# One slot of a software-pipelined attention, its groups of work in another order on five engines

## The reference

```python
x = x + xattn(layernorm(x), ctx)      # 16 heads of depth 32; q from x, k and v from ctx; softmax over 154
x = x + ffn(layernorm(x))             # 8 experts of 512x512; each token goes through its best 2
```

## Time and profile before

| | us |
|---|---|
| time, median of 3 runs | 1331.4 (1330.66 to 1331.42) |
| span of the profiled execution | 1340.9 |
| PE busy | 1224.7 (91%) |
| DVE busy | 881.3 (66%) |
| POOL busy | 744.6 (56%) |
| ACT busy | 722.1 (54%) |

### The profile page before, as it was taken

The page is one execution under the profiler, slowest core; times in us unless marked ns, Lnnn a source line. Parts: engine busy times, 40 slices in busy tenths (PEclk is TensorE's granted clock), DMA queues, the critical chain, the costliest instruction groups (busy, mean ns, idle before and its releaser), DMA issues. The chain is left out here.

```text
span 1340.9 us, 36001 instructions
## 1 busy us (share of the span) xinstructions
PE 1224.7 (91%) x11024; PEld 735.1 (55%) x11025; DVE 881.3 (66%) x1933; ACT 722.1 (54%) x1040; POOL 744.6 (56%) x980
## 2 busy tenths in 40 slices
PE   8887999998999989999999986869899999999997
PEld 4445665655655655665655654534354555555454
DVE  4657787877868867867877867545445555555454
ACT  4336875775775775775766662624333333334333
POOL 4003555675675675675675674864644445444545
PEclk9879999999989998989989997889999999999999
DMA  8842664584583574583583573967999989998886
GB/s 267 253 135 65 173 176 153 148 254 142 150 258 130 142 241 152 147 262 131 144 237 115 132 215 109 357 221 156 199 177 184 175 173 188 179 172 155 168 165 133
DMA packets 135547, 239.22 MB, mean 178 GB/s; under 512 B 18440, under 2 KB 49416, under 8 KB 134280
## 3 DMA queue, kind: packets, MB, share of 16 engines
q1 hardware_dynamic: 102391, 161.24, 41.2%
q0 software_dynamic: 29808, 67.73, 25.2%
q10 hardware_dynamic: 3232, 8.68, 1.9%
HBM read 112.00 MB, written 101.40 MB: 159 GB/s over the span
## 5 line engine op out<-in xcount | busy, mean ns | idle before, releaser
L1854 PE MATMUL S<-we_s,wq_s 128*128 x1620 | 376.3, 382 | 12.6 <-DVE att L1832 5.8
L1782 POOL DMA_INDIRECT out<-xn,to x135 | 208.9, 1547 | 212.7 <-DMA out<-xn,to 123.6
L1854 PEld LDWEIGHTS S<-we_s,wq_s 128*128 128x128 f16 x1620 | 158.1, 98 | 180.8 <-issue 22.3
L1172 POOL TENSOR_TENSOR we_s<-P_s,we_s 128x1024 f16<-128x1024 f32 x96 | 204.2, 2136 | 65.6 <-ACT we_s L927 65.3
L1793 ACT ACTIVATE wq_s<-PVp 128x512 f16<-128x512 f32 x137 | 81.6, 597 | 272.4 <-PE PVp L1844 247.1
L1252 POOL DMA_INDIRECT dispatched<-xn,idx x128 | 131.7, 1029 | 92.6 <-ACT xn L620 52.1
L975 DVE TENSOR_REDUCE mx_sb<-S 128x6 f32<-128x924 f32 x160 | 171.3, 1111 | 11.3 <-PE S L726 9.1
L708 PE MATMUL W<-we_s,wq_s 128*128 128x512 f16 x512 | 168.7, 409 | 8.7 <-ACT mT L933 5.3
L746 PE MATMUL W<-wo_s,aT_hi 128*128 128x512 f16 x512 | 164.5, 383 | 2.6 <-DVE aT_lo L953 1.4
L1832 DVE SCALAR_TENSOR_TENSOR att<-S,be_s 128x512 f32<-128x512 f32 x135 | 93.3, 691 | 111.0 <-PE S L1854 101.5
L1810 DVE TENSOR_TENSOR wq_s<-PVp,wq_s 128x512 f16<-128x512 f32 x137 | 94.6, 691 | 38.3 <-ACT wq_s L1793 35.1
(11 more groups left out here) (207 smaller groups left out, 2039.8 us busy)
## 6 DMA issues: line engine op xcount, KB each, us to landing
P_s<-dispatched SPq DMA_DIRECT2D x139, 260.5 KB
we_s<-we_s SPq DMA_DIRECT2D x186, 128.0 KB, 6.0
be_s<-in_x SPq DMA_DIRECT2D x16, 1024.0 KB, 9.1
xR_s<-in_x SPq DMA_DIRECT2D x16, 1024.0 KB
out<-xR_s SPq DMA_DIRECT2D x16, 1024.0 KB
...
```

Source lines behind the costliest of these rows:

```text
L1172: e.tensor_tensor(Pst[1][:, r:r + 2, :], exps(n), Pst[0][:, r:r + 2, :], ALU.subtract).then_inc(pldp, 1)
L1782: e.indirect_dma_start(out, bass.IndirectOffsetOnAxis(ap=to[u][:, :], axis=0), yw[u % YW], None, bounds_check=N - 1, oob_is_err=False, com ...
L1854: m = e.matmul(Yp[:, u % 2, :], gT[u % 2][xp][:, k, :], we_s[:, bass.ds(n * WN + (wp * KC + k) * D, D)], start=(c == 0), stop=(c == 11))
```

## The change

The five slot functions list the same calls in another order. No call is added or dropped, no helper, wait, buffer or bank is changed (`not b.last` has only gained brackets). The parts that the prediction speaks of:

```diff
 def pe_slot(e, s):
...
         if on_bm1:
             pe_PV(e, bm1, 6)
+            pe_PV(e, bm1, 7)
...
         if on_bm1:
             pe_AT(e, bm1, 0, s)
-            pe_PV(e, bm1, 7)
         if on_b:
             pe_ST(e, b, 3, s)
+            pe_ST(e, b, 4, s)
         if on_bm1:
             pe_AT(e, bm1, 1, s)
-        if on_b:
-            pe_ST(e, b, 4, s)
         if on_bp1:
             pe_LA(e, bp1, s)
+        if on_b:
+            pe_ST(e, b, 5, s)
         if on_bm1:
             pe_AT(e, bm1, 2, s)
             pe_AT(e, bm1, 3, s)
         if on_b:
-            pe_ST(e, b, 5, s)
             pe_PV(e, b, 0)
             pe_PV(e, b, 1)
...
         if on_bp2:
             pe_XT(e, bp2, 3, s)
-        if on_bm1 and not bm1.last:
+        if on_b:
+            pe_ST(e, b, 9, s)
+        if on_bp1:
+            pe_MX(e, bp1, 0, s)
+        if on_bm1 and (not bm1.last):
             pe_O(e, bm1, 3, s)
             pe_O(e, bm1, 4, s)
             pe_O(e, bm1, 5, s)
         if on_bp2:
             pe_Q(e, bp2, 0, s)
             pe_Q(e, bp2, 1, s)
-        if on_bp1:
-            pe_MX(e, bp1, 0, s)
...
             pe_MX(e, bp1, 4, s)
+        if on_b:
+            pe_PV(e, b, 4)
+        if on_bp1:
+            pe_MX(e, bp1, 5, s)
...
         if on_bp1:
-            pe_MX(e, bp1, 7, s)
-        if on_b:
-            pe_PV(e, b, 4)
-        if on_bp1:
             pe_MX(e, bp1, 8, s)
...
 def act_slot(e, s):
...
             act_EX(e, b, 2)
+            act_PH(e, b, 2)
         if on_bp1:
             act_Qh(e, bp1, 3)
...
+        if on_bp3 and (not bp3.first):
+            act_norm(e, 0, bp3)
+        if on_b:
             act_EX(e, b, 9)
             act_PH(e, b, 8)
             act_PH(e, b, 9)
-        if on_bp3 and not bp3.first:
-            act_norm(e, 0, bp3)
         if on_bp2:
             act_Qh(e, bp2, 0)
         if on_bp3:
             act_NX(e, bp3, 0)
-        if on_bp2:
-            act_Qh(e, bp2, 1)
-            act_WEh(e, bp2)
-        if on_bm2 and not bm2.last:
+            act_NX(e, bp3, 1)
+            act_NX(e, bp3, 2)
+        if on_bm2 and (not bm2.last):
             act_NY(e, bm2, 0)
...
 def dve_slot(e, s):
...
             dve_RB(e, bm3)
-        if on_bp2 and bp2.past(2):
-            dve_SA(e, bp2, 3)
-        if on_b:
-            dve_WEl(e, b)
+            dve_RM(e, bm3)
+        if on_b:
             dve_Ql(e, b, 2)
         if on_bm1:
             dve_PL(e, bm1, 1)
+        if on_bm2:
+            dve_NM(e, bm2, 3)
         if on_b:
             dve_Ql(e, b, 3)
...
 def sp_slot(e, s):
...
+        if on_bp3 and bp3.past(3):
+            sp_XA(e, bp3)
         if on_b:
             sp_KV(e, b)
-        if on_bp1:
-            sp_WL(e, bp1)
-        if on_bp3 and bp3.past(3):
-            sp_XA(e, bp3)
-        if on_b:
             sp_RS(e, b)
             sp_WW(e, b)
+        if on_bp1:
+            sp_WL(e, bp1)
```

More of the change, by code:

```diff
@@ L1429, in pe_slot @@
             pe_MX(e, bp1, 3, s)
-        if on_bm1 and not bm1.last:
-            pe_O(e, bm1, 6, s)
+            pe_MX(e, bp1, 4, s)
+        if on_b:
+            pe_PV(e, b, 4)
         if on_bp1:
-            pe_MX(e, bp1, 4, s)
+            pe_MX(e, bp1, 5, s)
         if on_bp2:
@@ L1482, in act_slot @@
         if on_b:
[L1483 removed]
+            act_EX(e, b, 3)
         if on_bm1:
@@ L1548, in dve_slot @@
         on_bm3, on_bm2, on_bm1, on_b, on_bp1, on_bp2 = bm3.here(), bm2.here(), bm1.here(), b.here(), bp1.here(), bp2.here()
-        if on_bm3 and not bm3.last:
+        if on_bm3 and (not bm3.last):
             dve_SN(e, bm3, 3)
@@ L1557, in dve_slot @@
         if on_bp2 and bp2.past(2):
+            dve_SA(e, bp2, 1)
             dve_SA(e, bp2, 2)
-        if on_bm3 and not bm3.last:
+        if on_bm3 and (not bm3.last):
             dve_RB(e, bm3)
-        if on_bp2 and bp2.past(2):
-            dve_SA(e, bp2, 3)
+            dve_RM(e, bm3)
         if on_b:
-            dve_WEl(e, b)
             dve_Ql(e, b, 2)
@@ L1571, in dve_slot @@
             dve_ATl(e, bm2, 0)
-            dve_NM(e, bm2, 3)
-            dve_ATl(e, bm2, 1)
         if on_b:
             dve_RA(e, b)
-        if on_bm3 and not bm3.last:
-            dve_RM(e, bm3)
         if on_bm2:
+            dve_ATl(e, bm2, 1)
             dve_ATl(e, bm2, 2)
@@ L1617, in dve_slot @@
         if on_b:
+            dve_DMX(e, b, 1)
             dve_DMX(e, b, 2)
+        if on_bm3 and (not bm3.last):
+            dve_RI(e, bm3)
+        if on_b:
             dve_DMX(e, b, 3)
@@ L1621, in dve_slot @@
             dve_DMX(e, b, 5)
+            dve_DMX(e, b, 6)
         if on_bp1:
@@ L1641, in pool_slot @@
             pool_PL(e, bp1, 2)
-        if on_bm1 and not bm1.last:
+        if on_bm1 and (not bm1.last):
             pool_RP(e, bm1)
+        if on_b:
+            pool_BX(e, b, 0)
         if on_bp1:
@@ L1650, in pool_slot @@
         if on_b:
-            pool_BX(e, b, 1)
             pool_BX(e, b, 2)
-        if on_bm1 and not bm1.last:
-            pool_RW(e, bm1)
         if on_bp1:
             pool_PL(e, bp1, 5)
+        if on_bm1 and (not bm1.last):
+            pool_RW(e, bm1)
         if on_bp4:
@@ L1665, in pool_slot @@
             pool_SC(e, bm1)
-        if on_b and not b.last:
+        if on_b and (not b.last):
             pool_NC(e, b, 1)
@@ L1676, in sp_slot @@
         on_bm2, on_b, on_bp1, on_bp3 = bm2.here(), b.here(), bp1.here(), bp3.here()
-        if on_bm2 and not bm2.last:
+        if on_bm2 and (not bm2.last):
             sp_XR(e, bm2)
-        if on_b:
-            sp_KV(e, b)
-        if on_bp1:
-            sp_WL(e, bp1)
         if on_bp3 and bp3.past(3):
@@ L1685, in sp_slot @@
         if on_b:
+            sp_KV(e, b)
             sp_RS(e, b)
             sp_WW(e, b)
+        if on_bp1:
+            sp_WL(e, bp1)
+        if on_b:
             sp_MR(e, b)
-        if on_bm2 and not bm2.last:
+        if on_bm2 and (not bm2.last):
             sp_XS(e, bm2)
```

77 lines of the change are left out of this document (37 added, 40 removed).

## The result

The changed kernel takes 1339.2 us (median of 20 runs, 1336.5 to 1349.5), the kernel before 1333.0 beside it (20 runs, 1326.8 to 1343.5). The ratio is 1.0049, 95% interval 1.0029 to 1.0069: slower by 0.5%, where 1296 us and faster were forecast.

The account below looks back on a forecast made before the run. PE was taken to bound every slot, losing time to waits and half clock. Terms -19.2 - 11.6 - 20.7 + 12.1 + 4.4 = -35.0 took 1340.9 to 1305.9 us profiled, 1296 as median; 8-in-10 range 1279 to 1322.

Parts of the forecast that it names:

- SC away from PV5: First scatter on POOL ends before PV5 starts, so LB's 15.7 and Q6's 3.5 us of waits go: -19.2 us.
- AT1 and AT2: Matmuls ST4 and ST5 moved over PE's two bank waits, for Ql3 and LA, remove them: -11.6 us.
- The clock: PE's half-clock stretches follow the waits; three quarters of the 27.6 us lost to them return: -20.7 us.
- POOL late: PL0 still stands behind the second scatter on POOL, so PV0 on PE waits 1.1 us a slot: +12.1 us.
- MX0 and the restack: MX0, 4.3 us earlier on PE, waits 0.4 us a slot for its restack's data: +4.4 us.
- MX0 waits for its restack: Rival, chance 0.12: restack issues late and lands slowly, PE stands 2.3 us a slot at MX0; slower, 1345 us.
- the stall only moves: Rival, chance 0.20: PV7 meets the second scatter, or SC slides; one stall of 1.7 us a slot returns; 1315 us.
- The rule of the Trainium skill: Rival, chance 0.13: scatter and PE are unrelated, late MT and clock stay, only AT's 11.6 us go; 1320 us.

Follow-up runs that it names:

- singles: Changed kernel with the second scatter's four indirect DMAs issued one by one (SD's place, behind PL0, PL2, RP): 1316.6 us, 0.9933 of the kernel before.
- Q: A chip without late completions; both kernels run again there: before 1283.5 us, changed 1308.1 us, ratio 1.0191.
- R: Another chip without late completions; changed kernel with the XA load behind the restack: 1292.6 us, 1.0054 of the kernel before.
- P: A chip with late completions; changed kernel with SD moved to POOL's gap ahead of RW: 1346.1 us, 1.0081 of the kernel before.
- S: A chip with late completions; kernel before (1323.9 us there) with SD moved to POOL's gap ahead of RW: 1377.4 us, 1.0409.

## Why the prediction was wrong

The forecast summed -35.0 us over the eleven slots; the profiles give -5.6, the medians no gain. By its own steps:

*SC away from PV5, -19.2*: right in mechanism and size; LB's and Q6's waits are gone. The reading of the cause, that the narrow PV matmuls stand still beside a scatter, is borne out in part: with no PV in SC's row nothing is late in ten of eleven slots, and in the eleventh, with PV4 in it, MX5 comes 1.8 us late. It isn't complete, since AT0 and ST3 come late in two slots where PV7 is done before SD begins.

*AT1 and AT2, -11.6*: **the step that failed.** AT2's 6.4 went. AT1's wait went from 5.2 to 20.5 us. The step counted the matmuls put over each wait and VectorE's queue, and never asked which of TensorE's completions the second scatter would make late. MTe came 2.4 us earlier, POOL's norm chain and SD with it, from +8.3 to +7.0, so SD now begins at PV7's end (323.89 against 323.94), with Q11 and everything for AT1 right behind it. With singles in SD's place AT1 waits 6.3 us in all, with SD moved away 6.3 to 6.5: 14 us of the 20.5 were the hold.

*The clock, -20.7*: PE busy fell by 6.0 (516.5 to 510.5), since as much idle time stayed in other places. Where nothing was held or waited for, PE needed 490.6 us for the same slots at 1.00: the clock's part had the right size for a cause that wasn't taken away.

*POOL late, +12.1*: 0.3 us seen. PL0 begins at +11.9 (reckoned +11.2), but PE, held at AT1, comes late too. Without a hold it shows: 5.9 us on Q. The kernel before pays 6.6 there in the same case, so even then it isn't the change's.

*MX0 and the restack, +4.4*: 0.4 seen, again hidden by AT1's wait; 9.9 once nothing is held. On Q, in the slot at 319.3, the first issue comes at +12.35 (reckoned +12.0), but the data is there only at +28.85 (348.17, where MX0 starts), 16.5 us later and not the 14.1 to 15.2 of the reckoning. The rival "MX0 waits for its restack" had the place right; it put PE's wait at 2.3 us a slot, and 0.9 was measured.

The rival that came nearest on the chips with a hold, "the stall only moves", saw the cause (SD meets PV7) and put it at 1.7 us a slot; the wait shows at AT1, 1.9 a slot (20.5 / 11). It still expected 1315 us, as it counted one stall of the old size back and left the rest of the gain, the clock's with it, standing. The rule of the Trainium skill ("SBUF — State Buffer", section "Who interferes with whom": "PE and ACT never wait on anyone") was to give 1320 us. It speaks of access to SBUF, and nothing here shows TensorE waiting for that; as a rule for engines as a whole it holds in the traces of Q and R and fails in those of P, S and the first profile, where TensorE's completions come late beside POOL's indirect DMAs, Q11's by 2.6 us (329.74 against 327.18).

Not settled: why the medians differ by 6.2 us where both hold. The last slot is 4.5 us longer after (59.6 against 826.8 - 771.7 = 55.1, idle 13.3 against 13.6, PEclk 0.83 against 0.88), and one profile a side can't say whether that repeats. Nor was it tried what in the chip makes the hold, or which matmuls beside a row bring it on.
